# Query/key items that lag behind their chunks, and ScalarE one-hots for five tiles

## The reference

```
xn = layernorm(x)
q, k, v = split(xn @ w_qkv.T); attn = q @ k.T / 4, masked where |i - j| > 128
attention = softmax(attn) @ v @ w_proj.T
affinity = sigmoid(xn @ router_w); top_w, top_idx = top 8 of 64, scaled to a sum of 1
shared = (silu(xn @ Wg) * (xn @ Wu)) @ Wd
routed = sum over the 8 experts e of token t: top_w * ((silu(xn @ G[e]) * (xn @ U[e])) @ D[e])
out = x + attention + shared + routed
```

## Time and profile before

| | us |
|---|---|
| median of 3 runs | 1360.69 (1357.23 to 1361.91) |
| the profiled execution | 1347.21 |
| its span, first to last instruction | 1345.4 |
| busy: PE, DVE, ACT, POOL | 1151.7, 764.0, 743.7, 637.9 |
| first `hots` starts, last one starts | 144.35, 212.13 |

### The profile page before, as it was taken

One profiled execution on the slowest core, in us unless ns is written; L12 is line 12 of the kernel. 1 busy time (PEld: TensorE's weight loads), 2 busy tenths in 40 slices (PEclk: granted clock), 3 DMA queues, 4 the chain that ended last, 5 costly groups with the idle time before them and its releaser, 6 DMA issues. The chain is left out here.

```text
span 1345.4 us, 31234 instructions
## 1 busy us (share of the span) xinstructions
PE 1151.7 (86%) x8297; PEld 822.5 (61%) x8298; DVE 764.0 (57%) x2405; ACT 743.7 (55%) x2023; POOL 637.9 (47%) x658
## 2 busy tenths in 40 slices
PE   7988995899998999998899988688888888878769
PEld 4544663778777877887777776344444444444347
DVE  7876993333333433343333356467767667777636
ACT  4554673555655656565555555356555555565443
POOL 1444104455455555545454543366656556665530
PEclk9999998899999999999999988789988889999889
DMA  7888222576667776676755553254455454555223
GB/s 241 219 211 228 95 94 69 170 205 207 204 208 205 222 206 206 198 216 196 207 167 172 167 156 105 78 141 128 126 139 129 119 144 124 135 137 143 80 64 110
DMA packets 143055, 214.30 MB, mean 159 GB/s; under 512 B 19441, under 2 KB 115698, under 8 KB 142962
## 3 DMA queue, kind: packets, MB, share of 16 engines
q1 hardware_dynamic: 70690, 84.16, 23.1%
q0 software_dynamic: 27648, 86.02, 23.0%
q10 hardware_dynamic: 44624, 43.00, 9.4%
HBM read 142.59 MB, written 70.26 MB: 158 GB/s over the span
## 5 line engine op out<-in xcount | busy, mean ns | idle before, releaser
L1120 POOL DMA_INDIRECT xb<-token_rows,idx_ring_x x320 | 303.1, 947 | 286.1 <-DVE ys L1271 198.9
L1912 POOL DMA_INDIRECT yg<-expert_rows,idx_ring x256 | 269.0, 1051 | 194.4 <-PE psum L1509 78.4
L1148 PE MATMUL psum<-xTe,wb_and_xT_all_or_onorm 128*128 128x128 f32 x2560 | 352.1, 281 | 10.1 <-issue 5.8
L1148 PEld LDWEIGHTS psum<-xTe,wb_and_xT_all_or_onorm 128*128 128x128 f32 x2560 | 316.0, 194 | 25.6 <-issue 14.0
L1677 ACT ACTIVATE wb_and_xT_all_or_onorm<-psum 128x384 f32<-128x384 f32 (+1 forms) x512 | 213.9, 472 | 185.8 <-PE psum L1509 150.1
L1271 DVE TENSOR_SCALAR ys<-psum,xb 128x256 f32<-128x256 f32 x320 | 154.4, 482 | 283.2 <-PE psum L1157 244.3
L1780 DVE CUSTOM_DVE_ANT_0 masked<-psum,mask_q 128x384 f32<-128x384 f32 (+1 forms) x480 | 233.6, 520 | 132.7 <-PE psum L1516 103.0
L1157 PE MATMUL psum<-wb_and_xT_all_or_onorm,aT 128*128 x640 | 201.1, 396 | 35.3 <-DVE ys L1271 26.7
L1524 PE MATMUL psum<-qk 98*128 98x384 bf16 (+1 forms) x512 | 171.0, 335 | 63.7 <-ACT wb_and_xT_all_or_onorm L1677 52.1
L1207 ACT COPY xTe<-psum 128x256 f32<-128x256 f32 x320 | 119.0, 372 | 182.3 <-PE psum L1138 139.4
L1221 ACT COPY wb_and_xT_all_or_onorm<-wb_and_xT_all_or_onorm 128x512 f32 x320 | 200.0, 626 | 18.2 <-SPq L1082 4.7
(11 more groups left out here) (149 smaller groups left out, 1183.7 us busy)
## 6 DMA issues: line engine op xcount, KB each, us to landing
expert_rows<-ys ACTq DMA_DIRECT2D x160, 256.0 KB
wb_and_xT_all_or_onorm<-in_w_exp SPq DMA_DIRECT2D x64, 384.0 KB
qk<-q_stacks SPq DMA_DIRECT2D x32, 384.0 KB
q_stacks<-wb_and_xT_all_or_onorm SPq DMA_DIRECT2D x32, 192.0 KB, 2.7
qk<-k_parts SPq DMA_DIRECT2D x32, 192.0 KB
k_parts<-wb_and_xT_all_or_onorm SPq DMA_DIRECT2D x28, 192.0 KB, 3.0
token_rows<-rows SPq DMA_DIRECT2D x8, 640.0 KB, 4.4
xb<-token_rows,idx_ring_x POOLq DMA_INDIRECT x320
```

What stands on the lines that cost most here:

```text
L1120: nc.gpsimd.indirect_dma_start(out=xb[:, r, :], out_offset=None, in_=rows_d, in_offset=bass.IndirectOffsetOnAxis(ap=idx_ring[:, q, r:r + 1 ...
L1148: last = nc.tensor.matmul(banks[GU + r % NB][:, part * P:(part + 1) * P], wgu[:, r % NW, h, part * I:(part + 1) * I], xT[:, r % NX, h, :], ...
L1912: nc.gpsimd.indirect_dma_start(out=yg[:, h, k, :], out_offset=None, in_=y_d, in_offset=bass.IndirectOffsetOnAxis(ap=idx_ring[:, h, k:k + 1 ...
```

## The change

Each chunk now gets three items (`EACH`), in order of their number, whichever chunk they belong to; the lag grows by one per chunk. Item 24 follows directly (`BETWEEN` = 25), and items 25 to 31 are done after the counts of the last chunk: their matmuls in TensorE's stream, their `leave` calls between the steps of VectorE's routing computation. All stores are SyncE's. GpSimd does two items, then the chunk's weights, then the third. VectorE's order inside a chunk is written anew: `affinities` no longer stands behind the first `leave`. The first two `product` calls move from before the maxima to behind the first two block tables. The lane table gets a buffer of its own (`hot_lanes`), and for tiles 1, 9, 17, 25 and 29 ScalarE makes it: eight activations Square(lane number - place), and one Relu(value - value x square), which is the token number at the right lane and zero elsewhere.

```diff
+    EACH = 3
+    NITEM = 4 * NCH
+    BETWEEN = EACH * NCH + 1
@@ scalar
         for c in range(NCH):
             take_vr(c, 0)
             if c > 0:
-                take_mid(c - 1, 3)
+                take_mid(items(c)[0] - 1)
             for t in range(1, TPC):
                 take_vr(c, t)
             add_one(c)
-            take_hi(c, 0)
-            take_mid(c, 0)
-            take_hi(c, 1)
+            first, second, third = items(c)
+            take_hi(first)
+            take_mid(first)
+            take_hi(second)
             if c + 1 < NCH:
                 copy_xT(c + 1)
-            take_mid(c, 1)
-            take_hi(c, 2)
-            take_mid(c, 2)
-            take_hi(c, 3)
-        take_mid(NCH - 1, 3)
+            take_mid(second)
+            take_hi(third)
+        for n in range(EACH * NCH, NITEM):
+            take_hi(n)
+            take_mid(n - 1)
+        take_mid(NITEM - 1)
@@ vector, a chunk without moments to come
-                leave(c, 0)
                 affinities(c)
                 if c > 0:
                     count(c - 1)
                 maxima(c)
-                leave(c, 1)
+                leave(first)
                 for t in range(TPC):
                     mark(c, t)
                 add_best(c)
                 choose(c)
-                leave(c, 2)
+                leave(second)
                 share(c)
-        leave(NCH - 1, 3)
+        for n in range(EACH * NCH - 1, BETWEEN):
+            leave(n)
@@ tensor
-            query_key(c, 0)
-            query_key(c, 1)
+            query_key(first)
+            query_key(second)
             if c + 1 < NCH:
                 transposes(c + 1)
-            query_key(c, 2)
-            query_key(c, 3)
-        ahead(pe)
+            query_key(third)
+        for n in range(EACH * NCH, BETWEEN):
+            query_key(n)
         count(NCH - 1)
+        for n in range(BETWEEN, NITEM):
+            query_key(n)
+            if n == BETWEEN + NQK - 1:
+                ahead(pe)
@@ route, vector
         for n in range(NTILE):
             c, t = divmod(n, TPC)
-            if n >= HB:
-                dve.wait_ge(lanes_scaled, n - HB + 1)
-            elif n == 0:
-                dve.wait_ge(lo_ready, NCH * 4)
-            one_hot(hot_l[:, n % HB, :, :], 0, n, P).then_inc(lanes_ready, 1)
+            if n not in FAR:
+                if n >= HB:
+                    dve.wait_ge(lanes_scaled, n - HB + 1)
+                one_hot(hot_l[:, n % HB, :, :], 0, n, P).then_inc(lanes_ready, 1)
@@ route, scalar
+        def far(n):
+            act.wait_ge(back_ready, 2)
+            if n >= HB:
+                act.wait_ge(lanes_scaled, n - HB + 1)
+            for k in range(K):
+                nc.scalar.activation(hot_l[:, n % HB, k, :], iota[:, 0:P], ACT.Square,
+                                     bias=lane_back[:, n * K + k:n * K + k + 1]).then_inc(far_ready, 1)
+            act.wait_ge(far_ready, K * fars(n))
+            if n >= HB:
+                act.wait_ge(hot_used, n - HB + 1)
+            nc.scalar.activation(hot_v[n % HB], hot_l[:, n % HB, :, :], ACT.Relu, bias=value[:, n:n + 1],
+                                 scale=value_back[:, n:n + 1]).then_inc(lanes_scaled, 1)
```

More of the change, by code:

```diff
@@ L144, in project, with items @@
     XT, QK, VR, CNT = 0, 2, 5, 7
+    EACH = 3
+    NITEM = 4 * NCH
+    BETWEEN = EACH * NCH + 1
+    def items(c):
+        return range(EACH * c, EACH * (c + 1))
     totals = banks[CNT][:, TPC * NE:(TPC + 1) * NE]
@@ L195, in sync, with store_item @@
         sp.dma_start(w_sh[:, :], w_exp[NE, :, :]).then_inc(shared_in, 16)
+        def store_item(n):
+            sp.wait_ge(lo_ready, n + 1)
+            store_part(sp, *divmod(n, 4))
         for c in range(NCH):
-            for o in range(2 if c == NCH - 1 else 4):
-                sp.wait_ge(lo_ready, c * 4 + o + 1)
-                store_part(sp, c, o)
+            for n in items(c)[:EACH - 1]:
+                store_item(n)
             sp.wait_ge(rows_ready, c + 1)
@@ L202, in sync @@
                          rows[:, c % NROWS, :, :]).then_inc(rows_out[c % NROWS], 16)
+            store_item(items(c)[EACH - 1])
+        for n in range(EACH * NCH, NITEM):
+            store_item(n)
     def scalar(act):
@@ L291, in gpsimd @@
                                     ALU.mult).then_inc(rows_ready, 1)
+            low(items(c)[EACH - 1])
+        for n in range(EACH * NCH, NITEM):
+            low(n)
     def vector(dve):
@@ L401, in normalise, with leave @@
                 done.then_inc(xn_ready, 1)
-        def leave(c, o):
-            n = c * 4 + o
+        def leave(n):
+            c, o = divmod(n, 4)
             dve.wait_ge(hi_ready, n + 1)
@@ L410, in leave @@
                                            ).then_inc(rest_ready, 1)
+        left["leave"] = leave
         def affinities(c):
@@ L467, in vector @@
         for c in range(NCH):
+            first, second, third = items(c)
             if c > 0:
-                leave(c - 1, 3)
+                leave(first - 1)
             if c + 1 < NCH:
@@ L700, in route, with fars @@
     G, NUMS, U, Y = 0, 2, 4, 6
+    def fars(n):
+        return sum(m <= n for m in FAR)
     def sync(sp):
@@ L704, in sync @@
             sp.wait_ge(parts_out[j], 16 * 16 * (NCH // 2))
-        for j in range(NROWS):
-            sp.wait_ge(rows_out[j], 16 * len(range(j, NCH, NROWS)))
-        sp.sem_inc(rows_stored, 1)
         for e in range(WARM):
@@ L747, in vector @@
         chain.wait()
+        leave, late = left["leave"], iter(left["late_items"])
+        leave(next(late))
         mine = slot[:, TPC:, :]
@@ L752, in vector @@
         dve.wait_ge(rows_ready, NCH)
-        for c in range(2):
-            product(c)
+        leave(next(late))
+        leave(next(late))
         for n in range(NTILE):
             chain.done(nc.vector.max(top8[:, n, :], slot[:, TPC + n, :]))
+            if n in (NTILE // 2 - 1, NTILE - 1):
+                leave(next(late))
         chain.wait()
@@ L765, in vector @@
                                          place_i[:, :, :].unsqueeze(3).to_broadcast([P, 2, NTILE * K, 2])))
+        nc.vector.tensor_scalar(lane_back[:, :], place_i[:, 0, :], -1.0, None, ALU.mult).then_inc(back_ready, 1)
+        for n in late:
+            leave(n)
         chain.wait()
@@ L789, in vector @@
             c, t = divmod(n, TPC)
[L790 to L794 removed]
+            if n not in FAR:
+                if n >= HB:
+                    dve.wait_ge(lanes_scaled, n - HB + 1)
+                one_hot(hot_l[:, n % HB, :, :], 0, n, P).then_inc(lanes_ready, 1)
             if n >= HB:
                 dve.wait_ge(hot_used, n - HB + 1)
[L797 to L798 removed]
+            elif n == 0:
+                for j in range(NROWS):
+                    dve.wait_ge(rows_out[j], 16 * len(range(j, NCH, NROWS)))
             one_hot(hot_b[:, n % HB, :, :], 1, n, NB_ROUTED).then_inc(blocks_ready, 1)
[L800 to L801 removed]
+            if n in (0, 1):
+                product(n)
+            elif t == 1 and 0 < c < NCH - 1:
+                product(c + 1)
             if n == TPC - 1:
@@ L875, in scalar @@
             c, t = divmod(n, TPC)
-            if n > 0:
+            if n in FAR:
+                far(n)
+            elif n > 0:
                 scale(n)
```

78 lines of the change are left out of this document (41 added, 37 removed).

## The result

| us | before | after |
|---|---|---|
| median | 1359.63 (1357.23 to 1361.91, 4 runs) | 1380.59 (1377.53 to 1390.38, 4 runs) |
| the profiled execution | 1347.21 | 1377.82 |
| its span | 1345.4 | 1375.9 |
| first `hots` starts, last one starts | 144.35, 212.13 | 143.68, 238.47 |
| busy: PE, DVE, ACT, POOL | 1151.7, 764.0, 743.7, 637.9 | 1164.0, 769.8, 755.2, 640.8 |

The account below looks back on a forecast made before the run. TensorE was taken as the bound nearly everywhere up to 213 us. First `hots` -7.8, tile 1 +1.3, tail -3.5, with 0.3 kept for small waits, gave -9.7: 1360.69 to 1351.0 us, range 1344.5 to 1359.

Parts of the forecast that it names:

- The one-hots: 32 tiles of one-hots: TensorE bound up to tile 24, then VectorE; 3.5 us gained, 1.3 us lost at tile 1.
- five rivals: Alternative outcomes: GpSimd holdup 15%, chunk period unchanged 7%, idle time nearly gone 17%, ScalarE tables late 10%, idle time exchanged 8%.
- the slower one: The rival, 7%, in which the chunk period does not fall and the kernel slows to 1367.8 us.
- signs of being wrong: Listed observations, among them chunk periods above 12.5 us, a late first table, and `hots` waiting for ScalarE's tables.
- The chunks: Projection chunks: mean period 11.7 us, last chunk starting 16.8 us earlier, 12.3 work put off and 4.5 idle time gone.
- The chain that I summed: VectorE's cycle through a chunk: 11.3 us in an even chunk, 12.0 in an odd one, mean 11.7.
- From the last chunk to the first `hots`: Routing stretch after the last chunk: 28.2 us of TensorE work plus waits, first `hots` at 136.5 us, 7.8 earlier.
- rival 1: Routing steps: GpSimd holds VectorE up, `product` 2.3 us later, gain only 7.4, 1353.3 us; chance 15%.
- full clock: First `down` runs at 2.4 GHz in 3.5 us instead of 5.2; if the clock falls again, 1.7 us go back.
- the tail: One-hots after tile 24: fewer lane tables on VectorE give 10.1 us instead of 12.7; 3.5 with 0.9 earlier idle time.
- rival 2: Projection chunks: period stays near 14 us, gain of 16.8 lost, kernel slower at 1367.8 us; chance 7%.
- the ring of three: Late items after the last counts: an item can run only three ahead of the `leave` calls, 0.6 us of waiting.

Follow-up runs that it names:

- e1: Kernel before with only the products of chunks 2 to 7 moved four block tables later: 1158.58 us, ratio 1.0192 to before.
- e2: Changed kernel with products 2 to 7 back at their places in the kernel before: 1137.57 us, ratio 1.0011 to before.
- e6: e4 with ScalarE's copies of the next chunk's turned rows ahead of the first `take_mid`: 1132.34 us, ratio 0.9969 to before.
- e7: e4 with GpSimd's third parts of the last eight items computed for 8 of 512 columns only: 1131.07 us, ratio 0.9963 to before.
- e3: Changed kernel without ScalarE's lane tables, products still late: 1156.92 us, ratio 1.0184 to before.
- e5: Changed kernel with the products of chunks 2 to 7 one block table earlier: 1137.51 us, ratio 1.0016 to before.
- e10: e2 with ScalarE's tables at tiles 9, 17 and 25 only: 1336.62 us, ratio 0.9981 to before.
- e8: Changed kernel with six useless matmuls ahead of each of the six product waits: 1220.91 us with other tokens, so read only before 230 us.
- e4: Changed kernel with products 2 to 7 back and no ScalarE tables: 1134.26 us, ratio 0.9982 to before.
- e9: e6 with `product(0)` ahead of block table 0 on VectorE instead of behind it: 1331.25 us, ratio 0.9946 to before.

## Why the prediction was wrong

**The failed step** is in the prediction's part "The one-hots". They were costed as untouched but for ScalarE's tables, and of the products only the first two were taken as moved. The diff moves eight: those of chunks 2 to 7 go four tables later, to the one place where their table and TensorE's `down` hang on the same `hots`. e1 and e2 show that this costs 22 us, the whole loss: the one-hots took 96.24 us where the forecast had 66.8 (69.03 + 1.3 - 3.5). Everything needed stood in the profile and the code: a block table of 1.5 us and a product of 0.6 behind a buffer that is given back by the very `hots` ahead of `down`, that is 2.1 us, six times; and 1.7 us of low clock behind a wait, as the earlier trace rows have it for the first `down`, came behind five of the six. None of the five rivals names it; the slower one bet on the chunk period. Of the signs of being wrong two came clearly, a first table more than 19 us after the last counts (129.28 - 109.68 = 19.6) and a wait of `hots` for ScalarE at tile 29; neither points at the products.

**The chunks.** The lag brought the last values from 109.87 to 97.58, 12.3 us earlier. Forecast were 16.8, of which 12.3 were work put off and 4.5 idle time gone. The work was put off; the idle time stayed for the most part, 5.05 us in the six chunks (73.89 - 68.84) instead of 6.56. The term that was mis-sized is the period, 12.3 and not 11.7 us. The chain that I summed was VectorE's alone. ScalarE's part was left out: in its stream the first `take_mid` waits for a `leave` that now stands behind the maxima, and `copy_xT` waits behind it:

```profile
59.58 0.62 ACT L253 CAST wb_and_xT_all_or_onorm<-rest 128x512 bf16<-128x512 f32 x1 [2.96 <-DVE rest L431]
...
60.59 1.00 ACT L222 COPY wb_and_xT_all_or_onorm<-psum 128x1024 f32<-128x1024 f32 x1
```

That is after, in chunk 3; TensorE's values of 61.65 above are what waits for this copy. e6 shows that 0.4 us of the period hang on its place.

**From the last chunk to the first `hots`.** VectorE took 129.28 - 111.87 = 17.4 us instead of 16.3. That is rival 1: GpSimd's work stretched the cast and a small operation (L767) by 1.0 us each ahead of the lane table, and the first block table behind it by 1.0; e7 shows it. I had given it 15% and put it down as an alternative to the forecast, where it was a cost that comes with every such order. The Trainium skill ("SBUF — State Buffer", on the shared port pair) says that the two engines exclude each other for a whole instruction in such operations. The rows agree: both sides grow, 3.84 us for two of GpSimd's at 129.48 and 2.44 for the table, and in e7 GpSimd's operation ends with VectorE's. The wait ahead of `down` was 2.06 us as forecast (some 2), but I took full clock behind it and it was low: 1.7 us, named and decided the wrong way for this trace (in e3, e5 and e6 the full clock held). `hots` 0 is 7.2 us late against the forecast. VectorE's stretch began 4.7 us late (111.87 against 107.2; 3.8 of it are the later counts), 1.1 were lost up to the lane table, 1.0 in the block table and 1.7 to the clock. That is 8.5 us; some 1.3 came back, mostly because the forecast had left 1.8 us between the end of that table and `down`, where 0.7 were enough.

**ScalarE's tables.** ScalarE's timeline at tile 1:

```profile
145.41 2.45 ACT L917 ACTIVATE hot_lanes<-iota,lane_back 128x128 f16<-128x128 f16 x8
147.90 1.24 ACT L922 ACTIVATE chosen<-hot_lanes,consts_f,value_back 128x1024 f16<-128x1024 f16 x1
```

Eight Squares take 2.45 us, 0.30 each. I had 1.5, between 1.4 and 2.3, and the higher end from the silu row was the nearer one. The Trainium skill ("VectorE: DVE Perf Modes", "The TRN2 errata") gives an estimate of 0.29 by its formula, and the trace agrees with it and not with my 0.19. So at tile 1 TensorE waited 2.64 us, not 1.3, and 1.7 us of low clock came behind it. With the five tables the tail gave back nothing (e2); with three it gave 0.6 us (e10). I had counted VectorE's saved tables and not ScalarE's 3.7 us at tile 29, which stop `hots` 29 for 2.2 to 2.3 us (e2, and L981 at 234.82 in after, where the profile names VectorE's table, but that had ended at 232.69 and the Relu ended at 234.68). e10 shows the cost of these two tiles. The forecast also took 0.9 us of idle time before tile 24 as won; it is 0.8 (55.12 us with 54.36 busy). And half of rival 2's 7% was entered as 0.02, where it is 0.035; nothing hangs on that.

**What was right:** that TensorE is the bound and its idle time is what counts; the wait ahead of the first `down`; that the ring of three makes the late items wait (0.83 and 0.42 us, forecast 0.6 in all); that the moved stores cost nothing visible. With the products back the forecast of -9.7 us would still have failed, at +1.1 (e2): the chunk period, the port, the clock and the tables take it.

Not settled: of the 30.6 us between the two profiled executions 26.5 are there at the end of the one-hots (239.92 against 213.38), and 4 more appear behind them, in code that is the same. No experiment looked at it. The profiled execution of before is also 10 us faster than any of its four timed ones, so these 4 us may be no more than that. The 26.5 lie inside the ratio's interval, 19 to 29 us, though above the 21.0 between the medians.

## What to carry to other kernels

When a step moves in a loop with a ring of buffers, write out for both ends which event frees the producer and which one starts the consumer: if both are the same event, the whole of what stands between is paid in every turn, and one step earlier it costs next to nothing (e5). Read every line of the diff that changes a condition or an index by what it does to each iteration, not only to the first. And an idle gap of TensorE can cost nearly twice its length where the clock falls behind it; useless work in the gap kept the clock (e8). Since the clock falls behind some gaps and not behind others of the same length, a difference of 1.7 us between two single traces proves nothing about an edit.

## What the runs showed of the hardware

- After waits of 2.06 to 3.43 us TensorE's next work often ran at 1.2 GHz, at a cost of 1.7 us each time: the first `down` in 5.2 instead of 3.5 us (after 2.06 us in after, 2.07 in e2, e4 and e10, and in the earlier trace rows 3.43), `hots` in 2.25 instead of 1.25 (after 2.18). It did not always: `down` took 3.5 us after the same 2.06 to 2.07 in e3, e5 and e6, and of the six waits for a late product, 2.18 us or more, one in after, one in e3 and two in e1 were followed by full clock. After waits of 1.79 (e9) and 0.83 us (e7) `down` took 3.5.
- VectorE's cast from int32 to fp16, 1024 wide, takes 0.71 us alone and 1.67 beside a GpSimd tensor_tensor; a 2560-wide fp16 compare 1.48 and 2.44. GpSimd's 8-column operation took 0.20 us alone and 1.53 beside VectorE's L786, and ended with it (e7). Such a hold-up lies inside the rows' durations and does not show as idle time.
- A ScalarE Square of 128 columns from SBUF to SBUF takes 0.30 us, hardly less than a silu out of PSUM (0.28).
